# A decoder layer on one core: other orders of work on ScalarE and VectorE, and the scaled delta written by ScalarE from PSUM

## The reference

```python
def step(Sm, inp):
    q_, k_, v_, g_, b_ = inp
    Sm = Sm * jnp.exp(g_)[..., None, None]
    kv = jnp.einsum('bhk,bhkv->bhv', k_, Sm)
    delta = (v_ - kv) * b_[..., None]
    Sm = Sm + jnp.einsum('bhk,bhv->bhkv', k_, delta)
    o = jnp.einsum('bhk,bhkv->bhv', q_, Sm)
    return (Sm, o)
...
og = o * jax.nn.silu(z)
var = jnp.mean(og * og, axis=-1, keepdims=True)
on = og * jax.lax.rsqrt(var + EPS) * norm_w
return on.reshape(B, S, VAL_DIM) @ w_out
```

## Time and profile before

| | us |
|---|---|
| median of three runs | 3695.97 (3694.45 to 3705.48) |
| the profiled execution | 3699.39 |
| its span | 3697.6 |

### The profile page before, as it was taken

The page is one execution under the profiler, slowest core; times in us unless marked ns, Lnnn a source line. Parts: engine busy times, 40 slices in busy tenths (PEclk is TensorE's granted clock), DMA queues, the critical chain, the costliest instruction groups (busy, mean ns, idle before and its releaser), DMA issues. The chain is left out here.

```text
span 3697.6 us, 75469 instructions
## 1 busy us (share of the span) xinstructions
PE 3171.6 (86%) x27888; PEld 2381.9 (64%) x27888; DVE 2802.7 (76%) x6451; ACT 1711.3 (46%) x5514; POOL 903.5 (24%) x1345
## 2 busy tenths in 40 slices
PE   1899999889999989989999989898989898428789
PEld 0777777777777777767777767676767776313344
DVE  4677777777777777777777777777777777599985
ACT  3445545454555554545455555455545554222221
POOL 0112222112222222222122212122222221365541
PEclk6899999999999999999999999999999998668999
DMA  5332322222323232322232323232223321200000
GB/s 221 95 91 81 91 81 88 80 86 75 94 79 94 69 96 65 91 83 90 82 91 82 90 77 90 77 94 79 90 84 89 83 82 24 74 12 17 23 9 17
DMA packets 398221, 288.44 MB, mean 78 GB/s; under 512 B 230016, under 2 KB 361216, under 8 KB 379904
## 3 DMA queue, kind: packets, MB, share of 16 engines
q1 hardware_dynamic: 397856, 283.62, 25.5%
HBM read 232.84 MB, written 50.73 MB: 77 GB/s over the span
## 5 line engine op out<-in xcount | busy, mean ns | idle before, releaser
L928 DVE SCALAR_TENSOR_TENSOR conv<-xb,convw,conv 128x512 f32<-128x512 f32 x768 | 570.7, 750 | 69.6 <-ACT conv L654 51.3
L473 PE MATMUL bank<-wout,onT 128*128 128x512 f32 x1024 | 533.5, 646 | 17.0 <-issue 17.0
L494 PE MATMUL bank<-w_hi,x_hi 128*128 128x256 f32 x1024 | 323.2, 316 | 151.4 <-ACT conv L654 151.4
L485 PE MATMUL bank<-x_hi,w_hi 128*128 128x512 f32 x1024 | 431.5, 421 | 18.1 <-DVE w_lo L934 14.9
L985 POOL TENSOR_TENSOR small<-small,half 128x4 f32<-128x4 f32 x64 | 64.7, 1011 | 1496.9 <-DVE small L761 1496.9
L485 PE MATMUL bank<-x_hi,w_lo 128*128 128x512 f32 x1024 | 401.2, 392 | 0.0
L485 PE MATMUL bank<-x_lo,w_hi 128*128 128x512 f32 x1024 | 400.8, 391 | 0.0
L995 POOL TENSOR_SCALAR De<-Dl,small 128x128 f32<-128x128 f32 x512 | 356.5, 714 | 118.1 <-ACT Dl L607 118.1
L650 ACT ACTIVATE xb<-bank 128x512 f32<-128x512 f32 x256 | 151.1, 590 | 406.5 <-PE bank L485 218.9
L494 PEld LDWEIGHTS bank<-w_hi,x_hi 128*128 128x128 f32 x1024 | 216.3, 211 | 180.4 <-ACT conv L654 177.7
L918 DVE TENSOR_TENSOR acc<-bank,acc 128x512 f32<-128x512 f32 x256 | 172.3, 689 | 183.2 <-PE bank L473 181.2
(11 more groups left out here) (205 smaller groups left out, 7116.4 us busy)
## 6 DMA issues: line engine op xcount, KB each, us to landing
x_hi<-x_hi_scratch SPq DMA_DIRECT2D x64, 1024.0 KB, 5.0
x_lo<-x_lo_scratch SPq DMA_DIRECT2D x64, 1024.0 KB, 8.1
decay<-decay_scratch SPq DMA_DIRECT2D x64, 512.0 KB, 5.5
M_scratch<-M SPq DMA_DIRECT2D x128, 256.0 KB, 2.3
w_raw<-in_w_proj SPq DMA_DIRECT2D x64, 384.0 KB, 5.5
Tc<-T_scratch SPq DMA_DIRECT2D x64, 128.0 KB, 2.4
wout<-in_w_out SPq DMA_DIRECT2D x16, 512.0 KB, 3.2
xT<-in_x_chunks SPq DMA_DIRECT2D x1, 4096.0 KB, 12.7
```

The costliest lines, as they stand in the source:

```text
L473: mm = pe.matmul(banks[4 + b][:], lhsT=onT[:, j, b, :], rhs=t["wout"][:, j, :], start=j == 0, stop=j == 1)
L485: mm = pe.matmul(banks[j % 2][:].rearrange("p (b t) -> p b t", b=B), lhsT=t[f"w_{p}"][:, k, j, :], rhs=t[f"x_{q}"][:, k], start=i == 0, st ...
L494: mm = pe.matmul(banks[half][:, i * 256:(i + 1) * 256], lhsT=t[f"x_{p}"][:, k, b, :], rhs=t[f"w_{q}"][:, k, 4:6, :], start=n == 0, stop=n ...
L928: dve.scalar_tensor_tensor(out=y3, in0=xb[:, :, i:i + C], scalar=t["convw"][:, j, i:i + 1], in1=y3, op0=ALU.mult, op1=ALU.add).then_inc(on ...
```

## The change

Three things. De is no longer written by POOL from Dl: ACT writes it from PSUM right behind Dl, half by half, with the scale cfl = cf times last, a new small product on DVE in gram; POOL's delta is gone. On ACT, project 2 stands ahead of lengths, gate 0 ahead of normed, silu 1 and 2 behind normed, silu 3 behind join_a, and the splits are spread out. On DVE, decays of step r + 2 stands at the end of round r between out 1 and out 2, where decays of r + 1 stood at its start; factors comes directly after update; taps 3 comes between out 0 and out 1; split 0 follows y_part 1 and the last two splits end the round. PE's and SP's programs are unchanged. Left out of the diff below are the lists of semaphores (cfl is added, the unused cleared and U_diag go) and the tiles small0 and small1, 72 wide instead of 64.

```diff
@@ -262,6 +262,7 @@
     of = lambda s, n, w=8: small(s)[:, n:n + w]
     n2, r2, nk = (lambda s: of(s, 0)), (lambda s: of(s, 8)), (lambda s: of(s, 16, 4))
     cf, cum, ncum, wq, last = (lambda s: of(s, 24)), (lambda s: of(s, 32)), (lambda s: of(s, 40)), (lambda s: of(s, 48)), (lambda s: of(s, 56))
+    cfl = lambda s: of(s, 64)
     two = lambda name, s: t[f"{name}{s % 2}"]
     later = lambda s: 3 * (s // NC) + s % NC - 1
     solve_bank = lambda n: banks[2 + n % 2]
@@ -601,11 +602,17 @@
                 act.wait_ge(on["cf"], s + 1)
                 if s:
                     act.wait_ge(on["PD"], 2 * s)
-                    act.wait_ge(on["De"], 2 * s)
+                    act.wait_ge(on["SD"], 2 * s)
+                    act.wait_ge(on["ss"], s)
                 for i in range(4):
                     u = 4 * half + i
                     op = act.activation(Dl[:, u // HJ, u % HJ], banks[4 + half][:, i * C:(i + 1) * C], ACT.Copy, scale=cf(s)[:, u:u + 1])
                 op.then_inc(on["Dl"], 1)
+                act.wait_ge(on["cfl"], s + 1)
+                for i in range(4):
+                    u = 4 * half + i
+                    op = act.activation(De[:, u // HJ, u % HJ], banks[4 + half][:, i * C:(i + 1) * C], ACT.Copy, scale=cfl(s)[:, u:u + 1])
+                op.then_inc(on["De"], 1)
 
         def update(s):
             if s % NC:
@@ -700,18 +707,17 @@
                 update(r)
             if ahead:
                 silu(r + 2, 0)
+                project(r + 2, 2)
             if state:
                 lengths(r)
             if ahead:
-                project(r + 2, 2)
-                silu(r + 2, 1)
                 project(r + 2, 3)
-                silu(r + 2, 2)
+                gate(r + 2, 0)
             if state:
                 normed(r)
             if ahead:
-                gate(r + 2, 0)
-                silu(r + 2, 3)
+                silu(r + 2, 1)
+                silu(r + 2, 2)
             if state:
                 turn(r)
             if ahead:
@@ -720,12 +726,14 @@
                 split(r + 3, 0)
             if solve:
                 join_a(r + 1)
+            if ahead:
+                silu(r + 2, 3)
             if fresh:
                 split(r + 3, 1)
-                split(r + 3, 2)
             if solve:
                 join_b(r + 1)
             if fresh:
+                split(r + 3, 2)
                 split(r + 3, 3)
 
     def vector(dve):
@@ -764,6 +772,9 @@
             dve.tensor_copy(by2(cum(s)), tok[:, :, c, 0, h]).then_inc(on["cum"], 1)
             dve.wait_ge(on["r2"], s + 1)
             dve.tensor_tensor(by2(cf(s)), tok[:, :, c, 1, h], r2(s)[:, 0:4].unsqueeze(2).broadcast_to([128, B, HJ]), ALU.mult).then_inc(on["cf"], 1)
+            dve.wait_ge(on["cf"], s + 1)
+            dve.wait_ge(on["last"], 2 * s + 2)
+            dve.tensor_tensor(cfl(s), cf(s), last(s), ALU.mult).then_inc(on["cfl"], 1)
             dve.wait_ge(on["cum"], s + 1)
             dve.tensor_scalar(ncum(s), cum(s), -1.0, None, ALU.mult).then_inc(on["ncum"], 1)
             dve.tensor_scalar(by2(wq(s)), r2(s)[:, 4:8].unsqueeze(2).broadcast_to([128, B, HJ]), 1.0 / DH, None, ALU.mult).then_inc(on["wq"], 1)
@@ -935,8 +946,6 @@
 
         for r in range(-3, NS):
             state, solve, ahead, fresh = r >= 0, 0 <= r + 1 < NS, 0 <= r + 2 < NS, r + 3 < NS
-            if solve:
-                decays(r + 1)
             if state:
                 read(r)
             if solve:
@@ -948,33 +957,32 @@
             if state:
                 output(r)
                 update(r)
+                factors(r)
             if ahead:
                 taps(r + 2, 1)
-            if state:
-                factors(r)
-            if ahead:
                 taps(r + 2, 2)
-                taps(r + 2, 3)
             if solve:
                 x_part(r + 1, 0)
-            if fresh:
-                split(r + 3, 0)
-            if solve:
                 y_part(r + 1, 0)
                 x_part(r + 1, 1)
                 y_part(r + 1, 1)
+            if fresh:
+                split(r + 3, 0)
             if state:
                 out(r, 0)
+            if ahead:
+                taps(r + 2, 3)
             if fresh:
                 split(r + 3, 1)
             if state:
                 out(r, 1)
-            if fresh:
-                split(r + 3, 2)
+            if ahead:
+                decays(r + 2)
             if state:
                 out(r, 2)
                 out(r, 3)
             if fresh:
+                split(r + 3, 2)
                 split(r + 3, 3)
 
     def gpsimd(pool):
@@ -983,17 +991,6 @@
             if s >= 2:
                 pool.wait_ge(on["Vn"], 2 * (s - 2) + 2)
             pool.tensor_tensor(nk(s), n2(s)[:, 0:4], t["half"][:, 0:4], ALU.pow).then_inc(on["nk"], 1)
-
-        def delta(s):
-            for half in range(2):
-                pool.wait_ge(on["Dl"], 2 * s + half + 1)
-                pool.wait_ge(on["last"], 2 * s + 2)
-                if s:
-                    pool.wait_ge(on["ss"], s)
-                for i in range(4):
-                    u = 4 * half + i
-                    op = pool.tensor_scalar(De[:, u // HJ, u % HJ], Dl[:, u // HJ, u % HJ], last(s)[:, u:u + 1], None, ALU.mult)
-                op.then_inc(on["De"], 1)
 
         def factors(s):
             pool.wait_ge(on["f"], 4 * s + 4)
@@ -1020,9 +1017,6 @@
                 gram(r + 1)
             if ahead:
                 project(r + 2, 0)
-            if state:
-                delta(r)
-            if ahead:
                 project(r + 2, 1)
                 project(r + 2, 2)
                 project(r + 2, 3)
```

More of the change, by code:

```diff
@@ L32 @@
 TERMS = [(k, a, b) for k in range(KT) for a, b in (("hi", "hi"), ("hi", "lo"), ("lo", "hi"))]
-SETUP_SEMS = "d_first d_in d_scratch x_split ones zeroed cleared ab yrow exs w_plus ln gates cums others ends betas tokens tok_copied".split()
+SETUP_SEMS = "d_first d_in d_scratch x_split ones zeroed ab yrow exs w_plus ln gates cums others ends betas tokens tok_copied".split()
 ATTENTION_SEMS = """d_x d_w0 d_w1 d_conv d_decay d_ends d_wout d_M d_N d_T d_Tc
     w_hi w_lo proj halo xb y save tap silu z z_read
-    E last kq_turned K_read squares n2 r2 nk cum cf ncum wq gram M P v_turned Vn
-    base Tc Uc X Xc Y T64 U_diag Y4_read XF xf UF U_done
+    E last kq_turned K_read squares n2 r2 nk cum cf cfl ncum wq gram M P v_turned Vn
+    base Tc Uc X Xc Y T64 Y4_read XF xf UF U_done
     KS R QS O_state TR Dl De PD O_sum og SD S_first S_next ss f ron on on_turned onT out_proj acc""".split()
@@ L92, in decoder_kernel @@
                                  ("w_raw", 2, 6, 128), ("decay", HJ, B, C), ("E", HJ, B, C),
-                                 ("M", B, HJ, C), ("P0", B, HJ, C), ("P1", B, HJ, C), ("sums", 8), ("junk", 8, C), ("small0", 64),
-                                 ("small1", 64), ("K0", B, DH), ("K1", B, DH), ("Vn0", B, HJ, DH), ("Vn1", B, HJ, DH),
+                                 ("M", B, HJ, C), ("P0", B, HJ, C), ("P1", B, HJ, C), ("sums", 8), ("junk", 8, C), ("small0", 72),
+                                 ("small1", 72), ("K0", B, DH), ("K1", B, DH), ("Vn0", B, HJ, DH), ("Vn1", B, HJ, DH),
                                  ("ends0", HJ, B), ("ends1", HJ, B),
```

## The result

| | median us | ratio to before, 95% interval |
|---|---|---|
| before | 3700.72 | |
| changed | 3488.07 (3479.61 to 3489.95) | 0.9416 (0.9383 to 0.9449) |

The changed kernel is 5.8% faster; 3546 was predicted, in a range of 3475 to 3630. The profiled execution has a span of 3485.8 us against 3697.6.

What follows compares the result with a forecast made beforehand. PE was taken as nearest its limit, DVE close behind; four rounds of 189.5 us were to become 171.4 plus gaps and clock, 180.0, saving 150 us over 63 rounds: 3699.4 to 3549, or 3546 against the median; range 3475 to 3630.

Steps and rivals of the forecast that it cites:

- rival 1: Weight queue and late following round hardly show on PE, clock stays full: gain 222 us, time 3475; chance 0.15.
- C: Round with r modulo 4 = 3: 45.40 us before, predicted near 43.7 with a gap of 0.4.
- D: Round with r modulo 4 = 0, no state read: 42.90 us before, predicted near 41.8 with a gap of 0.3.
- Xc at x + 8.5, gap x - 21.7: DVE's path to y_part, x being the start of lengths: when Xc is ready, and PE's gap left per round.
- my allowance for late DMAs: Gap added for rounds with later DMAs: 0.4 us in C, 0.6 in A, bounds 0 and 1.5.
- The boundary: Weight splits queue at the end of A; PE waits 2.7 us for out 2, B starts 3.2 late (bounds 2.5 to 5).
- B: Round with r modulo 4 = 2, following the weight-loading round; 49.65 us before.
- B after the boundary: Splits 2 and 3 stand ahead of read on DVE, x is 24.2 to 24.4: gap 2.6 us.
- The clock: One half-clock stretch of PE in B after its 2.7 us gap: 1.5 us per four rounds.
- De: ACT writes it instead of POOL: eight activations, 2.2 us, costing nothing and gaining PE's wait for De.
- POOL and the taps: POOL took the SBUF collisions, so DVE's taps gain nothing from its freed reads: 0 in the sum.
- A: Round with r modulo 4 = 1, loads the next head's weights: 50.24 us before, predicted gap 0.6.

Runs made afterwards that it cites:

- e3: Changed kernel with taps 3 ahead of x_part again on DVE: 3669.57 us, 0.9882 of the kernel before.
- e2: Changed kernel with lengths ahead of project 2 again on ACT: 3600.12 us, 0.9731 of the kernel before.
- e5: Kernel before with ACT's new order alone, DVE's order and De on POOL as before: 3695.07 us against 3695.20, 0.9998.
- e12: Changed kernel with the two scans of decays moved to before y_part 0 and x_part 1 on DVE, splits unmoved: 3478.77 us, 0.9386.
- e7: Changed kernel with decays at the start of the round again, for step r + 1: 3527.77 us, 0.9549.
- e8: Changed kernel with the subtraction for w_lo on POOL instead of DVE, and ACT's split 1 directly after split 0: 3450.94 us, 0.9333.
- e4: Changed kernel with the first head's weights used for all heads, the other 15 heads' fetches and splits left out: 3416.33 us, 0.9229.
- e1: Changed kernel with POOL writing De from Dl again, all orders still changed: 3517.24 us, 0.9502.
- e6: Kernel before with De written by ACT from PSUM alone, both orders as before: 3691.08 us, 0.9991.
- e10: POOL does the w_lo subtractions, but its split 1 waits until DVE has copied U; ACT's split 2 precedes silu 3: 3470.53 us, 0.9348.

## Why the prediction was right, and where it was off

The direction, the mechanism and the range were right; the gain was 212 us by the spans where 150 had been summed. That the range held is in part luck: 3488 lies outside the forecast of 3500 to 3600 and inside the range only because it took in half of rival 1. Term by term, for four rounds:

- *Ordinary rounds.* Predicted C 43.7, D 41.8; measured 43.28 and 41.52 in the rounds shown, 43.70 and 41.58 in the mean. The mean of C hits the figure by one round of 48.08, which PE did in part at a lower clock; the median is 43.28. The formula (Xc at x + 8.5, gap x - 21.7) gave a gap of 0.4 in C with my allowance for late DMAs; in fact x sat at 21.76, held by projection 2, and the gap at 0.24. The allowance of 0.4 and 0.6 was mostly not needed: M's earlier start lets base begin right after taps 0. e3 confirms the slope (2.25 us of taps, 2.25 us of wait), e2 the branch in which gate waits for lengths, e5 that the old order has its limit one stage on.
- *The boundary.* Predicted: PE waits 2.7 us for out 2 and enters B 3.2 us late. Measured: it waits 1.64 us for out 2, 0.29 for U, some more for the squares, and project 0 starts at 8.76 us instead of 5.86: 2.9 late. The walk of DVE's and ACT's queues was right to 0.6 us at each step: the last fetch landed at +4.5, and split 3 ended at +5.4 where 5.5 was written. PE was ready for out 2 later than the walk had it, at +3.3 instead of +2.6. e12 and e7 show that the squares behind split 3 hold PE about as long when out 2 does not; with the squares early and only out 2 late, in e8 (where DVE has no splits), B is 2.2 us shorter.
- *B after the boundary.* Predicted 2.6 of gaps; measured 0.31 at gate and 0.92 at y_part, 1.2. Here the step failed that put M only 0.3 us earlier than before relative to PE. In the changed kernel's timeline of B (from 1306.22), shown below, with PE's own lateness taken off (1306.22 + 2.9), lengths starts at 22.96, not 24.3: DVE's end of the round ran 0.6 us ahead of my walk, because I had added up full durations (0.7 us for an out) where the trace starts the next one 0.6 us on, before the last has ended. The two last splits, which I had at 0.96 us each, took 1.81 together, until +7.2.

```profile
1332.08 0.31 ACT L633 ACTIVATE De<-O 128x128 f32<-128x128 f32 x1 [1.12 <-DVE O L893]
...
1335.64 0.39 PE L495 MATMUL bank<-w_hi,x_hi 128*128 128x256 f32 x1 [0.31 <-ACT conv L661]
...
1340.57 0.75 PE L379 MATMUL bank<-Xc,Uc 32*32 32x32 f32 x64 [0.92 <-DVE Xc L853]
```

- *The clock.* Predicted 1.5 us for a stretch at half clock in each B; the loop ran at a mean of 1.00. The wait of 1.64 us was, like the 1.66 of the earlier trace rows, not followed by one in the B shown. After the first two rounds of the loop only two show a clock below 1.00: the B from 416.85 (clock 0.97, 50.72 us) and the C from 995.98 (0.93, 48.08 us). This is the third mis-sized term, and I had overdrawn it by counting the gap at 2.7.
- *De.* Predicted as cover for free and its wait as the gain; e1 prices it at 29 us within the new order, e6 at nothing within the old.
- *POOL and the taps.* Predicted zero, and e6 agrees for POOL's De. The Trainium skill's rule that I had weighed (SBUF — State Buffer, "Who interferes with whom": whichever of the two starts first holds the shared port) did show itself, in e8 and e10: there POOL's longer instruction stood first and DVE paid, a copy of 0.16 us taking up to 1.72.

Sum: 180.0 predicted, 176.2 measured. With the B shown, 1.5 us of the difference are the clock, 1.4 B's gaps and 0.3 the boundary. Over all 15 Bs the mean is 48.02, so B makes 2.6 of the 3.8 us; A makes 0.4, D 0.2, C nothing, and the rest is the shorter first round of the loop (36.2 us). The result is near rival 1's 3475, yet not for its reason: the boundary did show on PE, e4 prices it at 72 us.

## What to carry to other kernels

Of a wait on the bounding engine, ask at once what that engine would meet at its next stage: write the next stage's input as "start of the shared step + so much", and the difference between the two expressions is the gain. Here it was 1.9 us a round of a 2.4 us wait, and nothing when ACT's order changed alone. Work in an in-order queue is cheapest in the engine's own short waits for the bounding engine: the same splits and scans cost 72 us where the changed kernel has them (against the run without splits) and 2 us in slots of 0.75 to 1.45 us.

## What the hardware showed

- The same wait of 2.49 us on PE was followed by slowed matmuls in one round and not in another (e3). A shorter one can be too: in the changed kernel's C from 995.98 PE stood idle for 1.38 us within y_part, for nothing that the profile shows, and the next 7 us had a granted clock of 0.57, most of them at the lower of its two levels. The matmuls behind the gap, and the two windows that follow:

```profile
1032.85 0.25 PE L379 MATMUL bank<-Xc,Uc 32*32 32x32 f32 x5 [1.38 <-issue]
...
1033.04:1040.00 6.96, 6.96 (x27) 3.77 (x24) 6.64 (x13) 1.22 (x2) 0.00 (x0) 0.57 0.02 7
1040.00:1044.06 4.06, 4.06 (x23) 1.82 (x22) 2.31 (x5) 0.59 (x1) 0.00 (x0) 0.90 0.01 2
```

- In e3 PE's busy time grew by 105 us at the lower clock, about half of a loss of 195.
- A subtraction of 128x768 on POOL (1.81 us, two inputs in SBUF) held up DVE's copies (0.16 to 1.72 us, 0.28 to 1.84 us) and its taps (three in 4.97 instead of 2.31 us), while POOL's operations of 0.6 us with one input hardly lengthened a tap (770 ns at most in the kernel before, 891 in e1, median 752 in both) but went up to 1349 ns themselves.
- In the changed kernel ACT's read of projection 1, now right behind its other work, takes 0.80 us (L657) where it took 0.60. What slows it was not tested; ACT had time to spare there.
